# Layer 0 of a two-layer block: the first attention written out by engine, f32 rows for the drives, and drives by TensorE in groups of three

## The chip, the cores and the metric

The kernel is one program on one core of a Trainium2 chip. A core has five engines that each work through a queue of their own and wait for one another by semaphores: TensorE (PE in the profile), VectorE (DVE), ScalarE (ACT), GpSimd (POOL), and SyncE (SP), which issues the DMAs. The metric is the time of one execution on the device, in microseconds (us), as the median of several runs. The two versions differ in the first half of the program only.

## The reference

The input x has 4 blocks (b) of 128 tokens with 128 features. Two layers follow each other, each with three residual parts. Only the first two parts of layer 0 bear on the change:

```
x = x + xattn(layernorm(x), ctx, ctx, Wq, bq, Wk, ..., Wo, bo)      # 16 heads of 8 features
    scores = Q K^T / sqrt(8);  masked: head i sees only the keys j with (j - i) % 16 == 0
    out = softmax(scores) V @ Wo.T + bo
x = x + ssm(layernorm(x), W_in, conv_w, conv_b, W_x, W_dt, b_dt, A_log, D, W_out)
    xi, res = split(x @ W_in);   u = silu(causal_conv4(xi) + conv_b)  # 256 channels
    dbc = u @ W_x                         # 8 columns for dt, 16 for B, 16 for C
    delta = softplus(dbc[dt] @ W_dt + b_dt)
    h[n] = exp(delta * A[n]) * h[n] + delta * u * B[n]        # 16 states n, along the tokens
    y = sum_n C[n] * h[n] + u * D;   out = (y * silu(res)) @ W_out
```

After them come a feed-forward part with ternary weights, and layer 1 with a gated cross-attention, a self-attention with a bias, and a quantised feed-forward part. Their code and order are the same in both versions.

## The kernel before, in words

All 512 tokens fit one core. Each engine's queue is written out in Python, in one function per engine, with a `wait_ge` on a named semaphore ahead of an instruction where it needs another engine's result. So the order on every engine is fixed by the code.

**First attention.** Because of the mask each head sees every 16th key of a block's context, 128 keys, so a block has 16 heads of 128 queries by 128 keys: four groups of four heads, and a group's scores ("strip", 128x512 f32) fill one bank of PSUM. A strip goes through six steps: PE makes the scores (`scores`, L1299), DVE takes the maximum of each head (L889) and subtracts it (`difference`, L897), PE turns the four heads (`turn_diff`, L1402), ACT takes the exponential (L578). When the four strips of a block are done, PE multiplies by the values and by ones (`heads`), ACT makes one over the sum by Ln and Exp (L584, L588), DVE scales (`scaled`, L884), PE projects, and DVE adds to x, normalises and so on. `attention(ph)` is one function per engine that both layers use; it counts steps t, one strip each, and stages are due at fixed distances (`LAG`, `VALUES`, `SCALE`, `PROJECT`, `ADD`, `RSTD`, `NORM`, `TURN`). In layer 0 PE makes two strips of scores at every second step, into a ring of five banks. Ahead of each block's `heads` it multiplies ones with ones six times (`keep_warm(FILLS["heads"], 5)`), whose result nothing reads. Convolution and gates of the SSM come from the table `CHANNELS` in steps 17 to 21 and behind the attention.

**From dbc to the first scan.** PE makes the 40 rows of dbc in bank 6 (dt, B and C). ACT copies the dt rows (L651), PE multiplies them with W_dt, ACT takes Abs with the bias b_dt, Exp and Ln, DVE adds the bias once more (L1022), makes delta (L1025) and delta times u (du, L1028). POOL makes delta and du of the second half of the channels (L485, L488). The rows of B are spread over 128 partitions by a product with a one-hot column. For that they are split in three bf16 parts, by ACT (L653) and DVE (L1017, L1018), while PE multiplies ones 16 times.

**The loop.** 16 states n times two halves hf of the 256 channels make 32 steps k. DVE scans along the tokens (L1054). The scan needs the decay exp(delta A[n]) from ACT (L690) and the drive delta u B[n] in a bank. The drive is made either by DVE, du times the spread rows of B (L1035), or by PE as four transposes (L1576) of du that ACT has scaled token by token, four instructions per state, into one of two buffers (L676). `BY_PE` names the states of the second kind: 4, 5, 7, 8, 9, 11, 12, 13, 15. POOL multiplies the state with C[n] (the read, L496), and PE adds that into y by a product with the identity (L1299).

## Time and profile before

| | us |
|---|---|
| median of 3 runs | 236.97 (236.45 to 237.11) |
| the profiled execution | 236.94 |
| its span (first to last instruction) | 235.1 |
| PE, DVE, ACT, POOL busy | 200.7, 172.6, 119.7, 88.3 |
| mean granted clock of PE | 0.977 |
| first attention, from the first maximum to the last scaled block | 11.2 to 52.2 |
| to the last row of dbc | 62.1 |
| to the first scan | 69.3 |
| to the last scan's end | 113.9 |

The stages follow one another: the convolution of a block needs its attention, dbc needs all of u, the loop needs dbc. Within a stage the engines pass strips or steps to one another. So a stage is read by itself: which engine has no idle time in it, and what ends the waits of the others. The granted clock is a share of full speed, 1.00 being 2.4 GHz and about half of it 1.2 GHz.

### The profile page before, as it was taken

The numbers are of one execution on the slowest core, as the hardware profiler recorded it, in microseconds if no ns is written. First come the engines' busy times: TensorE is split into PE (matmuls) and PEld (weight loads), VectorE is DVE, ScalarE is ACT, GpSimd is POOL, SyncE is SP. The second block draws the span as 40 slices with busy tenths as digits, with TensorE's granted clock in tenths as the row PEclk, the third lists the DMA queues.
The fourth block names the chain that finished last, engine by engine and source line by source line (L and its number), as shares of the span: only waits on it lengthen the run. The fifth ranks groups of instructions, "written<-read, shape, count | busy, mean of one in ns | idle before, by whom it ended". The sixth has DMA issues, their size and how long they took to land.

```text
span 235.1 us, 5061 instructions
## 1 busy us (share of the span) xinstructions
PE 200.7 (85%) x1868; PEld 141.3 (60%) x1868; DVE 172.6 (73%) x486; ACT 119.7 (51%) x292; POOL 88.3 (38%) x104
## 2 busy tenths in 40 slices
PE   8879998799997799999986679999988798876832
PEld 5568777688663245454463446867885776664421
DVE  2489485733399999999789879497775868816785
ACT  3343633435878897986065636335242344453431
POOL 7002408110047799998423064400002566522000
PEclk9999999999999999999999999999999999997696
DMA  6999950000079988300000001400000000000001
GB/s 213 389 427 409 418 242 4 3 0 0 8 216 377 233 96 96 56 1 0 0 3 0 0 0 50 133 0 3 0 0 3 0 4 3 3 3 3 0 0 45
DMA packets 9224, 20.23 MB, mean 86 GB/s; under 512 B 736, under 2 KB 5472, under 8 KB 8176
## 3 DMA queue, kind: packets, MB, share of 16 engines
q1 hardware_dynamic: 8912, 19.78, 27.2%
q8 instruction: 15, 0.25, 0.4%
q10 hardware_dynamic: 288, 0.13, 0.2%
q14 instruction: 9, 0.07, 0.1%
HBM read 17.52 MB, written 2.38 MB: 85 GB/s over the span
## 4 chain that ended last, share of the span: by engine, by line
PE 39%; POOL 17%; DVE 16%; issue 16%; ACT 7%; DMA 3%; SPq 1%; POOLq 0%; DVEq 0%; ACTq 0%
PE bank L1299 32%; POOL region L496 9%; POOL diff L520 6%; DMA ctx_T_sb<-ctx_T 3%; PE bank L1723 3%; PE bank L1402 2%; DVE diff L897 1%; DVE ext L1260 1%; DVE ext L1261 1%; DVE neg_max L889 1%; DVE region L1275 1%; PE bank L1316 1%; ACT region L676 1%; POOL region L485 1%; DVE region L1129 1%
## 5 line engine op out<-in xcount | busy, mean ns | idle before, releaser
L1054 DVE TENSOR_TENSOR_SCAN region<-region,bank 128x512 f32<-128x512 f32 x32 | 37.1, 1203 | 0.9 <-ACT region L690 0.8
L1299 PE MATMUL bank<-region,early_sb 128*128 128x512 f32 x64 | 33.8, 621 | 3.2 <-POOL region L496 2.1
L578 ACT ACTIVATE region<-bank 128x512 f32<-128x512 f32 x32 | 18.6, 594 | 21.7 <-PE bank L1402 21.5
L1299 PE MATMUL bank<-ones 128*128 128x256 bf16 x198 | 28.5, 300 | 1.1 <-POOL ones L432 1.0
L1299 PEld LDWEIGHTS bank<-ones 128*128 128x128 bf16 x198 | 20.6, 107 | 8.0 <-issue 2.2
L536 ACT ACTIVATE lnv<-mv,eps_col 128x1 f32<-128x1 f32 x24 | 7.0, 291 | 31.6 <-DVE mv L819 21.2
L690 ACT ACTIVATE region<-region,a_neg 128x508 f32<-128x508 f32 x32 | 21.1, 708 | 2.3 <-DVE region L1054 1.2
L1402 PE MATMUL bank<-early_sb,diff 128*128 128x128 f32 x128 | 18.8, 280 | 3.8 <-POOL diff L520 3.2
L1299 PE MATMUL bank<-ctx_T_sb,region 128*32 128x128 f32 (+1 forms) x160 | 20.7, 341 | 1.1 <-DMA ctx_T_sb<-ctx_T 0.7
L520 POOL TENSOR_TENSOR diff<-region,neg_max 128x512 f32<-128x512 f32 x15 | 15.5, 1044 | 12.4 <-DVE neg_max L908 12.4
L453 POOL TENSOR_TENSOR xb<-x,rows_sb 128x512 f32<-128x512 f32 x3 | 3.8, 1266 | 39.0 <-DVE x L1179 27.9
L1299 PEld LDWEIGHTS bank<-region,early_sb 128*128 128x128 f32 x64 | 9.8, 189 | 13.8 <-POOL region L496 13.0
L1402 PEld LDWEIGHTS bank<-early_sb,diff 128*128 128x128 f32 x128 | 14.0, 141 | 6.7 <-POOL diff L520 4.1
L908 DVE CUSTOM_DVE_ANT_0 region<-bank,region 128x128 f32<-128x128 f32 x64 | 14.4, 286 | 3.6 <-PE bank L1299 3.6
L1299 PE MATMUL bank<-k_T,region 32*128 32x128 f32 x256 | 15.1, 283 | 2.2 <-ACT k_T L550 1.0
L676 ACT ACTIVATE region<-region,b_tok 128x256 f32<-128x256 f32 x36 | 15.3, 495 | 2.5 <-PE bank L1576 2.5
L1299 PEld LDWEIGHTS bank<-region,ctx_sb 128*128 128x128 f32 x128 | 15.2, 192 | 1.9 <-issue 1.9
L1299 PEld LDWEIGHTS bank<-k_T,region 32*128 32x128 f32 x256 | 12.7, 186 | 5.3 <-ACT k_T L592 1.7
L1204 DVE COPY region<-bank 128x512 f32<-128x512 f32 x16 | 10.9, 686 | 6.6 <-PE bank L1723 6.5
L1299 PE MATMUL bank<-region,ctx_sb 128*128 128x128 f32 x128 | 15.6, 275 | 0.0
L1576 PEld LDWEIGHTS bank<-early_sb,region 128*128 128x128 f32 x72 | 9.0, 141 | 9.1 <-issue 8.1
L889 DVE TENSOR_REDUCE neg_max<-bank 128x4 f32<-128x512 f32 x16 | 10.3, 684 | 3.5 <-PE bank L1299 3.5
(234 smaller groups left out, 412.1 us busy)
## 6 DMA issues: line engine op xcount, KB each, us to landing
ctx_sb<-ctx SPq DMA_DIRECT2D x4, 1024.0 KB, 23.9
ctx_T_sb<-ctx_T SPq DMA_DIRECT2D x3, 1024.0 KB, 10.3
late_sb<-late SPq DMA_DIRECT2D x1, 2416.0 KB, 17.3
bias_scratch<-bias_vec SPq DMA_DIRECT2D x1, 2040.0 KB, 25.3
ctx_T_sb<-ctx_T SPq DMA_DIRECT2D x2, 512.0 KB, 5.9
diff<-c_scratch SPq DMA_DIRECT2D x4, 256.0 KB, 6.2
x<-c_scratch SPq DMA_DIRECT2D x4, 256.0 KB, 6.4
region<-bias_scratch SPq DMA_DIRECT2D x1, 1024.0 KB, 5.6
```

Source lines behind the costliest of these rows:

```text
L496: done(pool.tensor_tensor(read[:, k % 3, :], state[:, k % 3, :], c_rows(n), ALU.mult), "read")
L520: done(pool.tensor_tensor(diff[:, w % 4], neg_biased[:, t % 3], neg_max[:, w % 4, :, None].to_broadcast([P, HG, P]), ALU.subtract), "diff")
L578: done(act.activation(probs_T[:, w % (2 * NG)].rearrange("p h q -> p (h q)"), step_bank(w)[:, :], ACT.Exp, scale=1.0 if w < 16 else -1.0), ...
L676: ins = act.activation(du_B[:, i % 2, b].rearrange("p h c -> p (h c)"), du_T[:, b].rearrange("p h c -> p (h c)"), ACT.Copy, scale=b_tok[:, ...
L690: done(act.activation(dst, src, ACT.Exp, scale=a_neg[:, hf, n:n + 1]), "decay")
L889: done(dve.tensor_reduce(neg_max[:, w % 4, :], step_bank(w)[:, :].rearrange("p (h k) -> p h k", h=HG), AX, ALU.max, negate=True), "neg_max")
L908: ins = dve.tensor_tensor_reduce(neg_biased[:, t % 3, j, :], src[:, j, :], rel_bias[:, HG * g + j, :], -1.0, HIGHEST, ALU.add, ALU.min, ne ...
L1054: done(dve.tensor_tensor_scan(state[:, k % 3, :], decay[:, k % NDA, :], bank[3 + k % 3][:, :], 0.0, ALU.mult, ALU.add), "state")
L1204: done(dve.tensor_copy(p2_T[:, w % 4].rearrange("p c q -> p (c q)"), bank[4 + w % 2][:, :]), "p2T_sb")
L1299: return pe.matmul(dst, lhsT, rhs, start=start, stop=stop)
L1402: ins = pe.transpose(step_bank(w)[:, j * P:j * P + P], diff[:, w % 4, j, :], ident)
L1576: ins = pe.transpose(bank[3 + k % 3][:, b * P:b * P + P], du_B[:, BY_PE.index(n) % 2, b, hf, :], ident)
```

## The change

Three parts of layer 0 are changed; nothing behind the loop is.

**1. The first attention.** `attention(ph)` is split. `second_attention` is the old loop for layer 1. `first_attention` is written out on PE, ACT and DVE, call by call. The scores of a block are made four strips at a time (`scores(0, t, NG)`), into the banks of `FIRST_BANKS`, and as soon as all but the last two strips of the block before have been through ACT. The 24 fills ahead of `heads` are gone. Convolution and gates are made block by block (`convolved(b, hf)`, `gates(b)`, products of 128 columns), those of block 0 ahead of the last block's heads. The sums over weights come later, their maxima behind the attention.

On PE, where the scores of block 1 stand: `k_T` are the keys, `diff` is a strip less its maximum, `ones` are fills, `v_heads` the values. Before:

```order
L1299 MATMUL bank<-k_T,region 128x128 [waits s_probs_T_sb,s_q_heads,s_k_sb]
L1299 MATMUL bank<-k_T,region 128x128 x7
L1402 MATMUL bank<-early_sb,diff 128x128 [waits s_diff]
L1402 MATMUL bank<-early_sb,diff 128x128 x3
L1299 MATMUL bank<-ones 128x256 [waits s_q_heads]
L1299 MATMUL bank<-ones 128x256 x5
L1299 MATMUL bank<-region,v_heads 32x128 [waits s_ones_heads,s_v_sb,s_probs_T_sb]
L1299 MATMUL bank<-region,v_heads 32x128 x15
L1299 MATMUL bank<-region,ones_heads 32x128 x16
```

The same place in the changed kernel:

```order
L1503 MATMUL bank<-early_sb,diff 128x128 [waits s_diff]
L1503 MATMUL bank<-early_sb,diff 128x128 x3
L1384 MATMUL bank<-k_T,region 128x128 [waits s_probs_T_sb,s_v_sb,s_q_heads,s_k_sb]
L1384 MATMUL bank<-k_T,region 128x128 x15
L1384 MATMUL bank<-region,v_heads 32x128 [waits s_v_sb,s_ones_heads,s_probs_T_sb,s_q_heads]
L1384 MATMUL bank<-region,v_heads 32x128 x15
L1384 MATMUL bank<-region,ones_heads 32x128 x16
```

Sixteen products of scores (four strips) now stand in one piece ahead of the heads of the block before, where eight stood, and the fills between are gone.

**2. dt and the rows of B.** b_dt is added by PE: two products of the identity with the broadcast column of b_dt, 512 columns each, start the banks that the dt products then add to. One f32 copy of the 40 rows (`small`, DVE) takes the place of the copies and of the bf16 parts. delta is one instruction of DVE per half, max(dt, 0) + Ln(...) (`steps_of(hf)`); that of the second half stands inside the loop. On PE, from dbc to the loop, before (`bc_parts` is the tile of the three bf16 parts):

```order
L1299 MATMUL bank<-ones 128x256 x6
L1299 MATMUL bank<-region,late_sb 128x512 [waits s_dt_sb]
L1299 MATMUL bank<-region,late_sb 128x512
L1299 MATMUL bank<-ones 128x256 x16
L1299 MATMUL bank<-bc_parts,one_hot_b 128x512 [waits s_gate_sb,s_consts,s_bc_parts]
L1299 MATMUL bank<-bc_parts,one_hot_b 128x512 [waits s_gate_sb]
```

The same place in the changed kernel (`cols_sb` holds b_dt and the one-hot columns, `region` is `small`):

```order
L1384 MATMUL bank<-ones 128x256 x6
L1384 MATMUL bank<-cols_sb,early_sb 128x512 x2
L1384 MATMUL bank<-region,late_sb 128x512 [waits s_small,s_dt_bias]
L1384 MATMUL bank<-region,late_sb 128x512
L1384 MATMUL bank<-region,cols_sb 128x512 [waits s_gate_sb,s_consts]
L1384 MATMUL bank<-region,cols_sb 128x512 [waits s_gate_sb]
```

The two bias products stand between the fills and the dt products, and the dt products wait for the bias products' own semaphore.

**3. The loop.** DVE's drives are those of states 0 to 3, 7 and 11; PE's are the others: groups of three, three and four. The rows of B for states 0 to 3 are spread by f32 products (K = 32). For states 7 and 11 a DMA on SP's queue brings the row to all partitions, from the copy of B and C in DRAM, into `w_tmp` and `wq_rest`; DVE's drive then has both inputs in SBUF. The first four steps are taken in the order (0,0), (1,0), (0,1), (1,1) (state, half). On DVE, from dbc to the scan of step 3, before (L1035 are drives, L1054 scans):

```order
L1028 TENSOR_TENSOR region<-region 128x512 [waits s_u,s_delta]
L1035 TENSOR_TENSOR bank<-region,bank 128x512 [waits s_b_ps,s_du]
L1054 SCALAR_TENSOR_TENSOR region<-region,bank 128x512 [waits s_decay,s_drive]
L1035 TENSOR_TENSOR bank<-region,bank 128x512 [waits s_b_ps]
L1035 TENSOR_TENSOR bank<-region,bank 128x512 [waits s_b_ps,s_du_rest]
L1054 SCALAR_TENSOR_TENSOR region<-region,bank 128x512 [waits s_decay,s_drive]
L1035 TENSOR_TENSOR bank<-region,bank 128x512 [waits s_state,s_b_ps]
L1054 SCALAR_TENSOR_TENSOR region<-region,bank 128x512 [waits s_decay,s_drive]
L1035 TENSOR_TENSOR bank<-region,bank 128x512 [waits s_state,s_b_ps]
L1054 SCALAR_TENSOR_TENSOR region<-region,bank 128x512 [waits s_read,s_decay,s_drive]
```

The same place in the changed kernel (L1099 is delta, L1105 du, L1117 drives, L1139 scans):

```order
L1105 TENSOR_TENSOR region<-region 128x512 [waits s_u,s_delta]
L1117 TENSOR_TENSOR bank<-region,bank 128x512 [waits s_b_ps,s_du]
L1139 SCALAR_TENSOR_TENSOR region<-region,bank 128x512 [waits s_decay,s_drive]
L1099 SCALAR_TENSOR_TENSOR region<-bank,region 128x512 [waits s_sp_log,s_dt_ps]
L1117 TENSOR_TENSOR bank<-region,bank 128x512 [waits s_b_ps]
L1139 SCALAR_TENSOR_TENSOR region<-region,bank 128x512 [waits s_decay,s_drive]
L1117 TENSOR_TENSOR bank<-region,bank 128x512 [waits s_b_ps,s_du_rest]
L1139 SCALAR_TENSOR_TENSOR region<-region,bank 128x512 [waits s_decay,s_drive]
L1117 TENSOR_TENSOR bank<-region,bank 128x512 [waits s_state,s_b_ps] x2
L1139 SCALAR_TENSOR_TENSOR region<-region,bank 128x512 [waits s_read,s_decay,s_drive]
```

delta of the second half now stands behind the first scan, and two drives stand ahead of the scan of step 3, the second of them on the rows of state 2.

The diff, cut to its core:

```diff
+FIRST_BANKS = (0, 1, 2, 3, 4, 7, 0, 1, 2, 3, 4, 7, 1, 0, 2, 3)
...
-BY_PE = (4, 5, 7, 8, 9, 11, 12, 13, 15)
+def by_hand(t, stage):
+    b = due(t, stage)
+    return b if b is not None and b < BY_HAND else None
+BY_PE = (4, 5, 6, 8, 9, 10, 12, 13, 14, 15)
+BY_SPREAD = BY_B[:4]
+BY_ROWS = BY_B[4:]
+ROWS_AFTER = {5: 7, 9: 11}
...
+                if n in ROWS_AFTER:
+                    m = ROWS_AFTER[n]
+                    if m == BY_ROWS[0]:
+                        sp_.wait_ge(S["w_quant"], 3)
+                    sp_.dma_start(b_rows(m), bass.AP(c_dram, m * T, [[0, P], [1, T]])).then_inc(b_in[BY_ROWS.index(m)], 16)
             sp_.wait_ge(S["bias_sb"], 1)
...
-                    keep_warm(FILLS["heads"], 5)
+                if ph == 0 and b >= 1:
+                    pe.wait_ge(S["x_ready"], b)
                 pe.wait_ge(S["probs_T_sb"], 4 * v + 4)
...
+                if ph == 0 and b >= 1:
+                    pe.wait_ge(S["probs_T_sb"], t - 2)
+                    if b == 1:
+                        pe.wait_ge(S["v_sb"], 1)
                 elif ph == 1 and t == NG:
                     pe.wait_ge(S["probs_T_sb"], 16 + 1)
                 elif ph == 1 and t == NG + 2:
...
+            def first_attention():
+                scores(0, 0, NG)
+                turn_xn(0, 0, 2)
+                pe.wait_ge(S["k_sb"], 2)
+                done(mm(kv_bank(0, 1)[:, 0:P], C("bv").to_broadcast([P, P]), ident), "v_bias_ps")
+                turn_xn(0, 0, 3)
+                turn_values(0)
+                pe.wait_ge(S["xnT_sb"], NB)
+                done(mm(bank[5][:, P:T], E("wqT"), xn_T[:, P:T]), "q_ps")
+                keys_values(1)
+                turn_diff(0)
+                turn_diff(1)
+                turn_values(1)
+                turn_diff(2)
+                turn_diff(3)
+                scores(0, NG, NG)
+                heads(0, 0)
+                keys_values(2)
+                turn_diff(4)
+                turn_diff(5)
+                project(0, 0)
+                turn_values(2)
+                turn_diff(6)
+                scores(0, 2 * NG, NG)
+                keys_values(3)
+                turn_diff(7)
+                turn_diff(8)
+                turn_values(3)
+                turn_diff(9)
+                heads(0, 1)
+                scores(0, 3 * NG, NG)
+                turn_diff(10)
+                turn_diff(11)
+                project(0, 1)
+                heads(0, 2)
+                turn_xn(1, 1, 0)
+                turn_diff(12)
+                turn_diff(13)
+                convolved(0, 0)
+                turn_diff(14)
+                project(0, 2)
+                turn_diff(15)
+                convolved(0, 1)
+                weight_sums()
+                heads(0, 3)
+                turn_xn(1, 1, 1)
+                gates(0)
+                turn_xn(1, 1, 2)
+                convolved(1, 0)
+                project(0, 3)
+                convolved(1, 1)
+                gates(1)
+                convolved(2, 0)
+                gates(2)
+                turn_xn(1, 1, 3)
+                convolved(2, 1)
+                convolved(3, 0)
+                gates(3)
+                convolved(3, 1)
...
-            pe.wait_ge(S["bc_parts"], 2)
-            pe.wait_ge(S["consts"], 2)
+                done(mm(bank[4 + hf][:, :], ident, C("b_dt", hf).to_broadcast([P, T]), True, False),
+                     "dt_bias")
+            pe.wait_ge(S["dt_bias"], DH)
+            pe.wait_ge(S["small"], 1)
+            for hf in range(DH):
+                done(mm(bank[4 + hf][:, :], L("w_dt")[DT_AT:DBC, hf * P:hf * P + P], small[DT_AT:DBC, :], False, True), "dt_ps")
+            pe.wait_ge(S["consts"], 1)
...
             def spread_b(n):
-                i = BY_B.index(n)
-                if i >= 2:
-                    pe.wait_ge(S["drive"], DH * (i - 1) + (i == 2))
+                if n >= 2:
+                    pe.wait_ge(S["drive"], n + 1)
                 else:
-                    pe.wait_ge(S["gate_sb"], len(SSM_GROUPS))
-                done(mm(bank[spread_bank(n)][:, :], one_hot_b[0:3 * BC, n:n + 1].to_broadcast([3 * BC, P]),
-                        bc_parts[:, :]), "b_ps")
+                    pe.wait_ge(S["gate_sb"], DH + 1)
+                done(mm(bank[spread_bank(n)][:, :], C("one_hot", n)[B_AT:DT_AT].to_broadcast([BC, P]), small[B_AT:DT_AT, :]), "b_ps")
             def tokens_of_b():
...
-                n, hf = k // DH, k % DH
-                if k == 1:
+                n, hf = unit(k)
+                if k in (1, 2):
+                    spread_b(k + 1)
+                if k == 2:
                     turn_du(1)
-                if hf == 0 and n + 2 in BY_B:
...
-            for hf in range(DH):
+            def decayed(hf):
                 act.wait_ge(S["dt_ps"], hf + 1)
-                done(act.activation(sp[:, hf, 0, :], bank[4 + hf][:, :], ACT.Abs, bias=C("b_dt", hf)), "sp_abs")
-            for hf in range(DH):
-                act.wait_ge(S["sp_abs"], hf + 1)
-                link(act.activation(sp[:, hf, 2, :], sp[:, hf, 0, :], ACT.Exp, scale=-1.0))
-                done(act.activation(sp[:, hf, 1, :], sp[:, hf, 2, :], ACT.Ln, bias=1.0), "sp_exp")
+                link(act.activation(sp[:, hf, 0, :], bank[4 + hf][:, :], ACT.Abs))
+                done(act.activation(sp[:, hf, 2, :], sp[:, hf, 0, :], ACT.Exp, scale=-1.0), "sp_exp")
+            def logarithm(hf):
+                act.wait_ge(S["sp_exp"], hf + 1)
+                done(act.activation(sp[:, hf, 1, :], sp[:, hf, 2, :], ACT.Ln, bias=1.0), "sp_log")
+            decayed(0)
+            logarithm(0)
+            decayed(1)
...
-                link(dve.tensor_tensor(bc_rest[0:end, :], rest[0:end, :], bc_parts[0:end, :], ALU.subtract))
-                done(dve.tensor_copy(bc_parts[0:end, :], bc_rest[0:end, :]), "bc_parts")
-                dve.wait_ge(S["bc_parts"], 1 if end > BC else 2)
-            for hf in range(DH):
-                dve.wait_ge(S["sp_abs"], hf + 1)
-                done(dve.tensor_scalar(du[:, hf, :], bank[4 + hf][:, :], C("b_dt", hf), 0.0, ALU.add, ALU.max), "dt_base")
-            dve.wait_ge(S["dt_base"], 1)
-            dve.wait_ge(S["sp_exp"], 1)
-            done(dve.tensor_tensor(delta[:, 0, :], du[:, 0, :], sp[:, 0, 1, :], ALU.add), "delta")
+            done(dve.tensor_copy(small[B_AT:DBC, :], bank[6][B_AT:DBC, :]), "small")
+            weight_inverses()
+            def steps_of(hf):
+                dve.wait_ge(S["dt_ps"], hf + 1)
+                dve.wait_ge(S["sp_log"], hf + 1)
+                done(dve.scalar_tensor_tensor(delta[:, hf, :], bank[4 + hf][:, :], 0.0, sp[:, hf, 1, :], ALU.max, ALU.add),
+                     "delta_rest" if hf else "delta")
+            steps_of(0)
             dve.wait_ge(S["delta"], 1)
-            dve.wait_ge(S["u"], DH * (len(SSM_GROUPS) - 1) + 1)
+            dve.wait_ge(S["u"], DH + 1)
...
             def drive(k):
-                n, hf = k // DH, k % DH
-                dve.wait_ge(S["b_ps"], BY_B.index(n) + 1)
+                n, hf = unit(k)
+                if n in BY_SPREAD:
+                    dve.wait_ge(S["b_ps"], n + 1)
+                    b_of = bank[spread_bank(n)][:, :]
+                else:
+                    dve.wait_ge(b_in[BY_ROWS.index(n)], 16)
+                    b_of = b_rows(n)
                 if k >= 3:
                     dve.wait_ge(S["state"], k - 2)
-                done(dve.tensor_tensor(bank[3 + k % 3][:, :], du[:, hf, :], bank[spread_bank(n)][:, :], ALU.mult), "drive")
+                done(dve.tensor_tensor(bank[3 + k % 3][:, :], du[:, hf, :], b_of, ALU.mult), "drive")
             dve.wait_ge(S["du"], 1)
             drive(0)
             for k in range(NS * DH):
                 if k == 1:
+                    steps_of(1)
+                    drive(1)
+                elif k == 2:
+                    dve.wait_ge(S["du_rest"], 1)
                     drive(2)
-                    dve.wait_ge(S["du_rest"], 1)
-                    drive(1)
-                if k >= 2 and k + 1 < NS * DH and (k + 1) // DH not in BY_PE:
+                elif k == 3:
+                    drive(3)
+                if 3 <= k < NS * DH - 1 and (k + 1) // DH not in BY_PE:
                     drive(k + 1)
                 if k // DH in BY_PE:
                     dve.wait_ge(S["drive_pe"], DH * BY_PE.index(k // DH) + k % DH + 1)
                 else:
-                    dve.wait_ge(S["drive"], 3 if k == 1 else drives_before(k) + 1)
+                    dve.wait_ge(S["drive"], drives_before(k) + 1)
                 dve.wait_ge(S["decay"], k + 1)
                 if k >= 3:
```

## Rows read from the trace of the kernel before

**Rows 1.** Windows: length, busy PE, PEld, DVE, ACT, POOL; PEclk, DMA share, GB/s.

```profile
11.20:52.20 41.00, 36.85 (x590) 30.00 (x591) 28.37 (x63) 17.47 (x53) 10.29 (x15) 1.00 0.54 222
52.20:62.10 9.90, 9.39 (x71) 8.62 (x70) 2.23 (x9) 6.51 (x15) 0.74 (x2) 1.00 0.01 2
62.10:69.30 7.20, 7.17 (x38) 3.91 (x37) 6.27 (x11) 5.68 (x10) 1.32 (x1) 1.00 0.49 136
69.30:113.90 44.60, 40.75 (x158) 20.14 (x155) 43.76 (x45) 35.11 (x69) 39.81 (x33) 1.00 0.57 121
```

**Rows 2.** Groups by line, 11.2 to 52.2: count, busy us, mean ns, idle before.

```profile
L889 DVE TENSOR_REDUCE neg_max<-bank 128x4 f32<-128x512 f32 x16 | 10.3, 684 | 3.5 <-PE bank L1299 3.5
L897 DVE TENSOR_TENSOR diff<-bank,neg_max 128x512 f32<-128x512 f32 x16 | 10.2, 683 | 0.0
L578 ACT ACTIVATE region<-bank 128x512 f32<-128x512 f32 x16 | 9.2, 593 | 10.2 <-PE bank L1402 10.2
L1299 PE MATMUL bank<-ones 128*128 128x256 bf16 x24 | 3.3, 273 | 0.2 <-DVE x L952 0.2
```

**Rows 3.** DVE's timeline, the last scaling: start, us, idle before and releaser.

```profile
52.23 0.29 DVE L884 TENSOR_TENSOR attn_T<-bank,inv_sum 128x128 f32<-128x128 f32 x1 [3.40 <-ACT inv_sum L588]
```

**Rows 4.** PE's timeline, heads, turns, convolution; scores of layer 1.

```profile
32.90 1.08 PE L1299 MATMUL bank<-region,v_heads 128*32 128x128 f32 x32
38.07 1.04 PE L1402 MATMUL bank<-early_sb,diff 128*128 128x128 f32 x8
54.42 1.95 PE L1299 MATMUL bank<-region 128*128 128x128 f32 x16
179.31 1.17 PE L1299 MATMUL bank<-k_T,region 32*128 32x128 f32 x32 [0.37 <-ACT k_T L592]
```

**Rows 5.** Timelines from dbc to the first scan: PE, ACT, DVE, POOL.

```profile
62.77 1.98 PE L1299 MATMUL bank<-region,late_sb 8*128 8x512 f32 x4
63.93 0.69 ACT L656 ACTIVATE region<-bank,cols_sb 128x512 f32<-128x512 f32 x1 [0.49 <-PE bank L1299]
65.37 0.62 ACT L659 ACTIVATE region<-region 128x512 f32<-128x512 f32 x1
67.84 0.69 DVE L1028 TENSOR_TENSOR region<-region 128x512 f32<-128x512 f32 x1
67.98 1.68 POOL L485 TENSOR_TENSOR region<-region 128x512 f32<-128x512 f32 x1 [15.04 <-ACT region L660]
```

**Rows 6.** Timelines in the loop: DVE, ACT; last POOL reads, DVE's last product.

```profile
76.92 1.21 DVE L1054 TENSOR_TENSOR_SCAN region<-region,bank 128x512 f32<-128x512 f32 x1
78.63 1.21 DVE L1054 TENSOR_TENSOR_SCAN region<-region,bank 128x512 f32<-128x512 f32 x1
93.18 2.33 DVE L1054 TENSOR_TENSOR_SCAN region<-region,bank 128x512 f32<-128x512 f32 x2 [0.44 <-ACT region L690]
84.91 1.31 ACT L690 ACTIVATE region<-region,a_neg 128x508 f32<-128x508 f32 x2
90.78 1.71 ACT L676 ACTIVATE region<-region,b_tok 128x256 f32<-128x256 f32 x4 [1.73 <-PE bank L1576]
110.68 3.72 POOL L496 TENSOR_TENSOR region<-region,x 128x512 f32<-128x512 f32 x3 [0.43 <-DVE region L1054]
113.97 0.98 DVE L1060 TENSOR_TENSOR region<-region,x 128x512 f32<-128x512 f32 x1
```

**Rows 7.** Windows in layer 1, columns as in rows 1.

```profile
200.00:203.00 3.00, 2.17 (x39) 1.81 (x33) 2.22 (x17) 1.36 (x5) 1.52 (x2) 1.00 0.00 0
211.00:214.00 3.00, 1.13 (x7) 0.75 (x6) 2.23 (x9) 1.88 (x6) 0.00 (x0) 1.00 0.00 0
214.00:221.00 7.00, 5.74 (x22) 3.08 (x22) 3.94 (x16) 2.32 (x5) 1.26 (x1) 0.52 0.01 2
222.00:225.00 3.00, 0.98 (x9) 0.63 (x7) 3.00 (x6) 0.46 (x1) 0.00 (x0) 1.00 0.00 0
```

**Rows 8.** The turns (L1402) alone in a window of rows 7.

```profile
200.00:203.00 3.00, 1.16 (x9) 1.03 (x10) 1.00 0.00 0
```

497 lines of the change are left out of this document (262 added, 235 removed).

## The prediction

> **What bounds the kernel now.** I read the windows by stage first, since the stages of layer 0 follow one another. In the first attention DVE is busy 28.37 of 41.00 us, ACT 17.47, and PE 36.85 [rows 1], but 3.3 us of PE are the 24 fills [rows 2]. So no engine is full: a block goes round PE, DVE, PE, ACT, PE, and what costs is that the round is not overlapped enough. The last block's scaling waits 3.40 us for the end of that round [rows 3]. Up to dbc PE is the bound (9.39 of 9.90). From dbc to the first scan it is a chain over ACT and DVE of 7.20 us; PE's 7.17 there are mostly fills. In the loop DVE is busy 43.76 of 44.60 [rows 1]: 32 scans at a distance of 1.12 (two take 2.33, one 1.21), and 0.59 more wherever DVE makes the drive itself (76.92 to 78.63). The rest is waiting for a decay, such as 0.44 at 93.18 [rows 6].
>
> **First attention.** I walk the new order on paper, each instruction at the earliest time at which its queue and its waits allow, with the distances between starts in these rows, and 0.03 to 0.1 us for a hand-over. The longest path, from 11.2:
> - DVE does 8 maxima and differences at 0.60, places values twice (0.27) and does three query products of the same size (0.66, an estimate from these rows): 7.3, to 18.5 (0.68 each, the next starting 0.08 before the end [rows 2]). The heads of block 0 wait for all queries.
> - PE: heads of block 0, 2.0 (two groups like the 1.08 one), keys 1.0. ACT: two copies of keys 0.5, two exponentials 1.1. PE: four strips of scores 1.1 [rows 2, 4]. With hand-overs 24.5.
> - DVE two maxima and a difference 1.9; PE turns two strips and a block of values 1.1 (eight turns take 1.04), heads 2.0, scores 1.1, one strip turned 0.5; ACT two exponentials 1.1; PE heads of block 2, 2.2. To 34.7.
> - ACT Ln, Exp and a copy 0.8. PE convolutions, turns, projection and weight sums 3.5; heads of block 3, 2.2. To 41.4, scaled at 42.1.
>
> Before, the last block is scaled at 52.2: **-10.1**. The fills explain 3.3 at most; the rest is that scores come a whole block earlier. The weakest price is that ACT and PE keep up in the written order: if each of the three later blocks keeps half of its old wait, the gain is 5. That is the other end of this term.
>
> **To dbc.** PE's queue after the last heads: 24 products of convolution, 8 of gates, one projection, at 0.22 (two records each; 16 records take 1.95 [rows 4]) are 7.2, less what the walk starts earlier; the rows of dbc 1.7. From 42.4 to 51.3: 9.2 us after the scaling, where it was 9.9. **-0.7**.
>
> **dbc to the first scan.** The copy of dt on ACT goes; it is replaced by the f32 copy on DVE of the same length, hidden under PE's fills and bias products. The two bias products are on the path: f32, 512 columns, as the two dt products that take 1.98 [rows 5]. They start behind the fills (0.8), and the dt products wait for them: dt starts 2.7 after dbc, where it started 0.65 after. **+2.0**. Against that, ACT did both Abs ahead of the first Exp (63.93 to 65.37), and now does Abs, Exp, Ln of the first half at once: -0.8; and DVE's two L1022 and L1025 become one instruction, -0.4, which before hid under ACT in part. The sum is 8.0 instead of 7.2: **+0.8**. The bf16 split, and PE's 16 fills beside it, lay beside this chain (DVE's L1028 starts as soon as delta is there [rows 5]), so their removal gives nothing. If the bias products lay hidden, this term would be -1.2; if the f32 spread of B (two products, 2.0, as dt) came onto the path as well, +2.0: these are its ends.
>
> **The loop.** Count for DVE: 32 scans x 1.12 = 36.0; 11 drives behind the first scan x 0.59 = 6.5 (13, 7.6, before); delta of the second half 0.7. That is 43.2, where before counts 43.6 and took 44.6. So two drives less save 0.4 net of delta. But waits come:
> - Start. delta of the second half stands behind the first scan. POOL's du (1.3), its first read (1.24, on the same queue behind it), PE's product of y, the spread of state 2 queued behind that product on PE (0.9 each, as the dt products) and the drive on it follow one another, and step 3's scan stands behind that drive on DVE's queue. 5.2 us, against 4.3 that DVE has to do meanwhile: **+0.9**.
> - Groups. For a state driven by PE, ACT needs four scalings and two decays, 1.60 + 1.22 = 2.82 (1.71 and 1.31 less 0.1 where the next starts [rows 6]), and DVE needs 2.25 for its two scans. Each such state puts ACT 0.57 behind. At a state driven by DVE it wins back up to 2.2 (DVE 3.42, ACT 1.22), but only as far as two buffers of scaled du allow: at 90.78 it waits 1.73 for one [rows 6]. Before, the groups are two, three, three and one, with 0.8 of waits for decays; now three, three and four. ACT enters the first group late (it still copies du of the second half), so I get waits of 0.45, 0.55, 0.3, 0.3 and 0.75 at steps 8, 10, 18, 26 and 28: 2.4, **+1.6**.
> - The drives of states 7 and 11 have both inputs in SBUF. DVE's last product of the loop has them too: it started while POOL's last read had 0.43 to go and took 0.98, where the same form took 0.69 ahead of POOL; there POOL's L485 took 1.68, where three reads in a row take 3.72 [rows 5, 6]. So whichever comes second waits. POOL is busy 39.81 of 44.60 [rows 1]. Of the two drives of a state the first comes behind POOL's read, as the product at 113.97 did, and the second ahead of one, since scans are 1.71 apart there: 2 x 0.3 on DVE, **+0.6**; 0 if all come ahead, 4 x 0.9 if all come as POOL starts. The Trainium skill has this rule, "SBUF — State Buffer", "Who interferes with whom": a DVE instruction with two SBUF inputs and a GpSimd one that reads SBUF exclude each other, and the later one is held until the other is done. The trace agrees, with 0.98 for 0.69; by the rule alone a drive that starts with a read would be held for all of it, 4 x 1.2.
>
> In sum -0.4 + 0.9 + 1.6 + 0.6 = **+2.7**; the ends are -0.4 (all waits hidden) and +5.7. The B rows of those states come by two DMAs of 256 KB, queued after the C rows of states 5 and 9; the DMA share in the loop is 0.57 [rows 1] and they are wanted 15 us later: nothing.
>
> **Sum.** -10.1 - 0.7 + 0.8 + 2.7 = -7.3. Walked in the same way, the order of before ends its last scan 1.1 us early, so such a walk misses waits; of that I give back 0.4. -6.9 against the profiled execution's own 236.94 (span 235.1 and 1.8 around it) is 230.0; the median shown is 0.03 higher. **230.0**. Behind the loop the order is the same, so a shift there stays a shift.
>
> **Rivals.**
> 1. The clock falls at the loop's start. PE has only fills and then a wait of about 2.5 us for the first read. The clock fell to 0.52 behind a stretch with PE busy 1.13 of 3.00, but stayed at 1.00 in one with 0.98 [rows 7], so the rows bear out either. At half speed the products of y and the turns of du take twice as long until it rises: +1.7, 231.7. Chance 0.25.
> 2. The attention keeps half of its waits (5 instead of 10.1): 235.1. For it: one late strip now delays a whole block of scores. Against it: each wait above has a price in the rows. Chance 0.13.
> 3. Slower: the clock stays low in the attention. On the path above PE does 16.7 us; at half speed as much again, less what it hides, +14.5: 244.5. It decides from about half of the attention on, since 6.9 of 14.5 eats the whole gain. Against it, the 33.5 us of real work, now in 30, leave PE no emptier than before, when the clock was 1.00 throughout [rows 1]. Chance 0.04. The Trainium skill has a rule for it, "TensorE: Matmul & The Clock Gate", "Part 4: PE-mode transpose": transposes do not count as activity in the way that products do. By it the turns here (64 instructions), with no fills between them, would not hold the clock, and the time would be that of this rival. The trace speaks against it: from 200 to 203 the turns are 1.16 of 2.17 us of work, and the clock is 1.00 [rows 7, 8].
> 4. Nothing changes, because something else ends the attention, such as the context's DMAs. But no wait of PE on a DMA stands in its window; 237.0, chance 0.02.
>
> **Numbers.** Likeliest case 0.56, with 228.4 to 231.4 as its own range (half of the way to the ends of the dt and loop terms); rivals 0.25, 0.13, 0.04, 0.02. The range that holds 8 in 10 takes in the first two cases, with room below for waits that are hidden and above towards the second rival: 227.8 to 232.9. A measurement of this kernel can tell 0.3% (0.7 us). Faster 0.94, same 0.02, slower 0.04.
>
> **What would show it.** The last block's scaling near 42.1; dbc near 51.3; the first scan near 59.3, with PE's two 512-column bias products right ahead of dt; the last scan's end near 107, with DVE waiting for ACT's decays in groups of three and at step 3 for a drive. It is wrong if the granted clock falls below 1.00 before 60, if the four scalings stand as far apart as before, or if the loop takes less than before's 44.6.

## The result and the profile after

The changed kernel takes 235.32 us (median of 20 executions, 231.38 to 238.18), the kernel before 237.13 (20 executions, 236.18 to 241.73). The ratio is 0.985 (95% interval 0.981 to 0.988); it leaves out the executions that count as slow, 11 of the 20 of the changed kernel, which the medians keep (by them it is 0.992). So the changed kernel is faster by more than the noise, but by less than 2%: the medians differ by 1.8 us where 7 were forecast, and 235.32 lies above the range, which ended at 232.9. The profiled execution took 234.37 (span 232.6). By stage, with a second execution of the same kernel that is told of below (run a_5):

| us | before | forecast | after, profiled (234.37) | a_5 (236.44) |
|---|---|---|---|---|
| first maximum starts at | 11.2 | 11.2 | 12.0 | 11.3 |
| to the last scaling of the attention | 41.0 | 30.9 | 31.9 | 32.4 |
| to the rows of dbc | 9.9 | 9.2 | 9.6 | 9.6 |
| to the first scan | 7.2 | 8.0 | 8.2 | 8.2 |
| to the last scan's end | 44.6 | 47.3 | 48.3 | 52.0 |
| from there to the end | 121.2 | 121.2 | 122.6 | 121.3 |

The windows of the changed kernel for the stages of [rows 1], columns as there (length; busy PE, PEld, DVE, ACT, POOL; granted clock; DMA share and GB/s):

```profile
12.00:43.90 31.90, 28.72 (x558) 24.29 (x558) 26.75 (x62) 17.65 (x51) 5.69 (x8) 1.00 0.67 277
43.90:53.40 9.50, 9.26 (x74) 8.52 (x74) 3.34 (x10) 6.41 (x13) 5.36 (x9) 1.00 0.01 2
53.40:61.60 8.20, 6.95 (x28) 3.36 (x28) 3.12 (x7) 4.12 (x9) 0.00 (x0) 1.00 0.48 153
61.60:109.90 48.30, 42.77 (x164) 21.19 (x164) 44.41 (x44) 36.33 (x74) 41.09 (x32) 1.00 0.55 117
```

In the attention DVE is now busy 26.75 of 31.90, where it was 28.37 of 41.00: nearly the same work, with 5.2 us of waits in place of 12.6. The clock stays at 1.00 with the fills gone. In the loop DVE has only 0.65 more to do, and waits 3.9 instead of 0.8. DVE's timeline there (start, length, line, form, and in brackets the idle time ahead and what ended it):

```profile
67.01 0.68 DVE L1117 TENSOR_TENSOR bank<-region,bank 128x512 f32<-128x512 f32 x1
68.24 0.70 DVE L1117 TENSOR_TENSOR bank<-region,bank 128x512 f32<-128x512 f32 x1 [0.56 <-PE bank L1384]
68.84 1.21 DVE L1139 TENSOR_TENSOR_SCAN region<-region,bank 128x512 f32<-128x512 f32 x1
...
74.42 2.33 DVE L1139 TENSOR_TENSOR_SCAN region<-region,bank 128x512 f32<-128x512 f32 x2 [0.36 <-DVE bank L1117]
77.24 2.33 DVE L1139 TENSOR_TENSOR_SCAN region<-region,bank 128x512 f32<-128x512 f32 x2 [0.48 <-issue]
80.05 3.44 DVE L1139 TENSOR_TENSOR_SCAN region<-region,bank 128x512 f32<-128x512 f32 x3 [0.48 <-PE bank L1707]
83.41 1.00 DVE L1117 TENSOR_TENSOR bank<-region,w_tmp 128x512 f32<-128x512 f32 x1
...
91.31 3.44 DVE L1139 TENSOR_TENSOR_SCAN region<-region,bank 128x512 f32<-128x512 f32 x3 [0.73 <-ACT region L723]
...
102.55 2.33 DVE L1139 TENSOR_TENSOR_SCAN region<-region,bank 128x512 f32<-128x512 f32 x2 [0.73 <-ACT region L723]
105.37 4.55 DVE L1139 TENSOR_TENSOR_SCAN region<-region,bank 128x512 f32<-128x512 f32 x4 [0.48 <-PE bank L1707]
```

Three kinds of loss stand in these lines: the drive that waits for the spread of state 2 (68.24), waits of scans from step 6 on, most of them inside the groups of PE's states (74.42, 77.24, 80.05, 91.31, 102.55 and 105.37, that is steps 6, 8, 10, 18, 26 and 28: 3.3 in sum), and a drive of 1.00 with both inputs in SBUF (83.41), which takes 0.67 elsewhere. The tail behind the loop has the same order as before, but takes 1.4 longer in this execution; its clock is 0.86 between 130 and 140 us, and of the traces of this order those without that fall, and without another ahead of 200 us, have tails of 120.9 to 121.3.

### The profile page after: what moved, and what is told of

It reads as the page before. It is cut to its first block, busy times and chain, and to the rows that moved or that the text cites. A ratio compares the mean times of both kernels' runs of the same rounds, so it can differ in the third digit from the quotient of the medians.

```text
span 232.6 us, 5040 instructions
## 1 busy us (share of the span) xinstructions
PE 196.0 (84%) x1857; PEld 137.4 (59%) x1857; DVE 169.6 (73%) x480; ACT 119.7 (51%) x290; POOL 88.2 (38%) x103
## 4 chain that ended last, share of the span: by engine, by line
PE 39%; issue 19%; POOL 19%; DVE 13%; ACT 4%; DMA 3%; SPq 1%; POOLq 0%; DVEq 0%; ACTq 0%
PE bank L1384 31%; POOL region L506 12%; POOL diff L530 6%; DMA ctx_T_sb<-ctx_T 3%; PE bank L1854 3%; PE bank L1503 3%; DVE ext L1345 1%; DVE ext L1346 1%; PE bank L1405 1%; ACT region L748 1%; DVE region L1214 1%; DVE region L1360 1%; DVE region L909 1%; ACT region L788 1%; DVE region L1189 1%
## 5 line engine op out<-in xcount | busy, mean ns | idle before, releaser
L1139 DVE TENSOR_TENSOR_SCAN region<-region,bank 128x512 f32<-128x512 f32 x32 | 37.2, 1203 | 3.4 <-ACT region L723 1.5
L1384 PE MATMUL bank<-region,early_sb 128*128 128x512 f32 x64 | 34.3, 623 | 5.5 <-POOL region L506 4.0
L1384 PE MATMUL bank<-ones 128*128 128x256 bf16 x158 | 23.5, 309 | 2.3 <-ACT b_tok L727 1.3
L1384 PE MATMUL bank<-ctx_T_sb,region 128*32 128x128 f32 (+1 forms) x160 | 21.8, 346 | 2.3 <-DMA ctx_T_sb<-ctx_T 1.6
L1384 PEld LDWEIGHTS bank<-ones 128*128 128x128 bf16 x158 | 16.7, 110 | 7.5 <-ACT b_tok L727 2.1
L530 POOL TENSOR_TENSOR diff<-region,neg_max 128x512 f32<-128x512 f32 x15 | 15.5, 1044 | 12.4 <-DVE neg_max L942 12.4
L709 ACT ACTIVATE region<-region,b_tok 128x256 f32<-128x256 f32 x40 | 16.9, 495 | 2.9 <-PE bank L1707 2.9
L1707 PEld LDWEIGHTS bank<-early_sb,region 128*128 128x128 f32 x80 | 9.9, 141 | 10.6 <-issue 10.3
L1289 DVE COPY region<-bank 128x512 f32<-128x512 f32 x16 | 10.9, 685 | 7.1 <-PE bank L1854 6.9
L1249 DVE TENSOR_REDUCE row_max<-bank 128x1 f32<-128x512 f32 x16 | 10.9, 688 | 2.5 <-PE bank L1384 2.3
L788 ACT ACTIVATE region<-bank,shift 128x512 f32<-128x512 f32 x16 | 10.8, 686 | 3.0 <-DVE shift L1256 3.0
## 6 DMA issues: line engine op xcount, KB each, us to landing
late_sb<-late SPq DMA_DIRECT2D x1, 2416.0 KB, 17.6
```

The lines of the kernel that those rows point to most:

```text
L530: done(pool.tensor_tensor(diff[:, w % 4], neg_biased[:, t % 3], neg_max[:, w % 4, :, None].to_broadcast([P, HG, P]), ALU.subtract), "diff")
L709: ins = act.activation(du_B[:, i % 2, b].rearrange("p h c -> p (h c)"), du_T[:, b].rearrange("p h c -> p (h c)"), ACT.Copy, scale=b_tok[:, ...
L788: done(act.activation(p2[:, b % 2, g, :], bank[g][:, :], ACT.Exp, bias=shift[:, b:b + 1], accum_out=part_sum[:, b, g:g + 1]), "p2")
L1139: done(dve.tensor_tensor_scan(state[:, k % 3, :], decay[:, k % NDA, :], bank[3 + k % 3][:, :], 0.0, ALU.mult, ALU.add), "state")
L1249: done(dve.tensor_reduce(row_max[:, b, g:g + 1], bank[g][:, :], AX, ALU.max), "row_max")
L1289: done(dve.tensor_copy(p2_T[:, w % 4].rearrange("p c q -> p (c q)"), bank[4 + w % 2][:, :]), "p2T_sb")
```

## The experiments

"First six steps" is the time from the start of scan 0 to that of scan 6 (11.0 us before, 12.8 in the profiled execution after); "steps 6 to 31" that from the start of scan 6 to that of scan 31 (32.4 and 34.3).

**The fills of before** (b_nofills):

```diff
-                    keep_warm(FILLS["heads"], 5)
```

> The kernel before without the 24 fills ahead of the heads; nothing else. If the attention's gain comes from the order (four strips of scores in one piece), the stretch from the first maximum to the last scaling loses at most the fills' own 3.3 us of 41, so it stays above 37.7. If the fills were what cost, it falls near the changed kernel's 31.9. If they held the clock, the granted clock falls to about half between 12 and 50 us and the stretch grows by 10 or more.

Measured, one execution: 244.68, with the first maximum at 14.0 (late DMAs) and 44.0 us for the attention instead of 41.0. The clock was 0.5 between 10 and 20, behind a wait of PE for the late DMAs, and 0.74 between 45 and 50: it fell at 47.4, in a wait of PE of 1.97 us ahead of a block's heads, where six fills stood before. So taking the fills out does not bring the old order near 31.9: 9.5 us of the stretch ran at half speed, and with half of that given back it would still take 39.2 (an estimate). The gain of the attention is the order's, but for what the fills' own 3.3 us may be worth. What the fills cost or hold in the old order can't be told from this execution: b_nocover below, which keeps them, started as late (13.4, at half speed until 17.6) and took 42.8.

**The start of the loop** (a_start):

```diff
-            keep_warm(FILLS["dt_in"], 1)
             for hf in range(DH):
                 done(mm(bank[4 + hf][:, :], ident, C("b_dt", hf).to_broadcast([P, T]), True, False), "dt_bias")
-            pe.wait_ge(S["dt_bias"], DH)
-            pe.wait_ge(S["small"], 1)
-            for hf in range(DH):
+                pe.wait_ge(S["dt_bias"], hf + 1)
+                pe.wait_ge(S["small"], 1)
                 done(mm(bank[4 + hf][:, :], L("w_dt")[DT_AT:DBC, hf * P:hf * P + P], small[DT_AT:DBC, :], False, True), "dt_ps")
...
-                if k in (1, 2):
-                    spread_b(k + 1)
+                if k in (0, 1):
+                    spread_b(k + 2)
```

> The changed kernel with two orders on PE altered: no fills ahead of the bias products and bias, dt, bias, dt instead of bias, bias, dt, dt; and the rows of states 2 and 3 spread one product of y earlier. If the bias products and the fills are on the path as I priced them, dbc to the first scan falls from 8.18 to about 6.2. If the spread behind the first product of y holds step 3, the distance from step 2's scan to step 3's falls from 2.97 to about 1.9. Rival: both only wait for something else (POOL's du, ACT's Exp) and neither stretch changes by over 0.3. If the fills held the clock, it falls below 1.00 between 54 and 66.

Measured: 232.92; dbc to the first scan 6.75 (1.4 less, where 2.0 were expected), step 3 after 2.31 instead of 2.97 (0.66 less, where 1.1 were). So both stretches are on the path, at some two thirds of the price. But the clock was 0.50 from 64 to 70, and step 5 came after 5.29 instead of 1.71; since this run also lacks the fills ahead of the bias products, it can't tell whether they had held it.

**The port of SBUF** (a_spread): states 7 and 11 spread by PE at steps 10 and 18.

```diff
-BY_SPREAD = BY_B[:4]
-ROWS_AFTER = {5: 7, 9: 11}
+BY_SPREAD = BY_B
+ROWS_AFTER = {}
+SPREAD_AT = {10: 7, 18: 11}
```

> The changed kernel with the rows of B of states 7 and 11 spread by PE into a bank, as those of states 0 to 3, instead of by DMA into SBUF: their four drives have one input in SBUF. If the port of SBUF shared by VectorE and GpSimd is the cause, the two drives of 1.00 go back to 0.68 and POOL's reads beside them lose no 0.95 each; the loop then falls from 48.3 by 0.6 (the drives alone) to 2 (if POOL's 1.9 are on the path). Rival: PE is the bound in the loop, and two products of 0.9 more on PE make it longer by 0.5 to 1.8.

Measured: 237.44; the clock fell at the loop's start again (0.5 from 63.9 to 77.6, first six steps 17.1). Behind it, steps 6 to 31 take 33.6 instead of 34.3. POOL's timeline of the changed kernel, and of this one:

```profile
83.82 3.43 POOL L506 TENSOR_TENSOR region<-region,k_T 128x512 f32<-128x512 f32 x2
```

```profile
86.21 1.28 POOL L508 TENSOR_TENSOR region<-region,k_T 128x512 f32<-128x512 f32 x1
87.67 1.27 POOL L508 TENSOR_TENSOR region<-region,k_T 128x512 f32<-128x512 f32 x1 [0.19 <-DVE region L1141]
```

The same two reads take 3.43 in one piece there, and 1.28 and 1.27 here, and the first drive of a state goes from 1.00 to 0.67. So each side is held by the other, as the Trainium skill has it ("SBUF — State Buffer", "Who interferes with whom"). On the path it is 0.7, close to the 0.6 forecast.

**A third buffer of scaled du** (a_buf3):

```diff
-        du_B = turn("ssm", [2, NB, DH, P])
+        du_B = turn("ssm", [3, NB, DH, P])
...
-                if i >= 2:
-                    act.wait_ge(S["drive_pe"], DH * (i - 1))
+                if i >= 3:
+                    act.wait_ge(S["drive_pe"], DH * (i - 2))
```

> The changed kernel with three buffers of scaled du instead of two. If ACT's waits of 1.48 at 88.9 and 100.2 for a buffer are what make DVE wait 0.73 at 91.3 and at 102.6, those go and the loop falls from 48.3 to 46.9 or less; DVE's waits at steps 8 and 10 (0.48 each) stay, since there ACT is late from the start. Rival: ACT's 2.82 us per state against DVE's 2.25 is the bound whatever the buffers, and the waits only move: the loop changes by less than 0.5.

Measured: 236.85, the clock at 0.66 between 65 and 80 (first six steps 15.5). Steps 14 to 31 take 21.64 instead of 22.68, steps 6 to 13 are unchanged at 11.6: the buffers' waits were real, and are 1.0.

**The unchanged changed kernel again** (a_again five rounds, a_third, a_4, a_5, a_6 one execution each).

> The changed kernel unchanged, to see a second trace of it and its times beside the next two on one chip. If the clock at the loop's start is what spreads its times (231.4 to 238.2), times lie in two bands some 3 us apart, and a trace of the upper band shows the granted clock at 0.5 between 60 and 75 us and 15 to 17 us for the first six steps, one of the lower band 1.00 and 12.8. Rival: the spread comes from the start (DMA landings, 1 to 2 us) or from the tail's clock, and the first six steps are 12.8 in either.

> The changed kernel unchanged once more, one execution, for its trace. If the clock at the loop's start makes the upper band of its times, this execution is either near 232 with 12.8 us for the first six steps, or near 235 to 238 with the granted clock at 0.5 between 60 and 80 and 15 to 17 us for them. Rival: a time near 235 or above with 12.8 and a clock of 1.00 there.

> The changed kernel unchanged, one execution. Theory: executions above 235 have the granted clock at 0.5 somewhere between 60 and 80 and 15 or more for the first six steps; those below have 12.8. Rival: the upper band comes from the tail's clock (130 to 230) and the start alone, with 12.8 in each.

> As the run before it: above 235 only with a fall of the clock between 60 and 80, by the theory; above 235 with 12.8 us for the first six steps, by the rival.

> As the two runs before it: a third execution for the same question.

Measured: a_again 235.53 (median of 6, 232.15 to 241.47; before 238.30 on that chip, ratio 0.980, 0.971 to 0.989). The traced executions took 232.15, 233.30, 236.63, 236.44 and 233.07. In those of 232.15, 233.30 and 233.07 the first six steps take 12.8 and the clock is 1.00 there; in those of 236.63 (a_4) and 236.44 (a_5) they take 15.3 and 16.5, and the clock falls. The windows of the profiled execution first, then those of a_5:

```profile
64.00:66.00 2.00, 0.00 (x0) 0.00 (x0) 1.94 (x3) 1.84 (x4) 2.00 (x3) 1.00 1.05 363
66.00:70.00 4.00, 3.97 (x8) 1.18 (x8) 3.44 (x5) 0.00 (x0) 2.44 (x2) 1.00 1.05 393
70.00:76.00 6.00, 5.29 (x19) 2.34 (x19) 5.64 (x8) 5.07 (x11) 4.09 (x4) 1.00 0.92 185
```

```profile
64.00:66.00 2.00, 0.23 (x1) 0.23 (x2) 1.97 (x3) 1.59 (x3) 2.00 (x3) 1.00 1.03 370
66.00:70.00 4.00, 4.00 (x5) 1.07 (x5) 2.12 (x4) 0.00 (x0) 2.19 (x2) 0.55 1.05 397
70.00:76.00 6.00, 6.00 (x11) 2.26 (x10) 3.88 (x6) 1.64 (x4) 2.54 (x2) 0.50 0.91 167
```

PE is idle or nearly so from 64 to 66 in both; in a_5 the clock is then at half speed, PE is full, and DVE and ACT wait for it (3.88 and 1.64 busy of 6.00, where they are 5.64 and 5.07). What PE does in that stretch of a_5 is the chain on the path (products of y, the spreads of states 2 and 3, the turn of du):

```profile
65.78 1.50 PE L1384 MATMUL bank<-region,early_sb 128*128 128x512 f32 x2 [2.37 <-POOL region L506]
67.20 2.07 PE L1384 MATMUL bank<-region,cols_sb 32*128 32x512 f32 x2
69.20 2.08 PE L1384 MATMUL bank<-region,early_sb 128*128 128x512 f32 x2
71.21 2.07 PE L1384 MATMUL bank<-region,cols_sb 32*128 32x512 f32 x2
73.21 1.12 PE L1698 MATMUL bank<-early_sb,region 128*128 128x128 f32 x4
```

The same products in the profiled execution:

```profile
66.03 1.12 PE L1384 MATMUL bank<-region,early_sb 128*128 128x512 f32 x2 [2.37 <-POOL region L506]
67.08 1.12 PE L1384 MATMUL bank<-region,cols_sb 32*128 32x512 f32 x2
```

Each pair takes 2.07 where it takes 1.12 at full speed. Behind the same wait of 2.37 the clock falls or does not: it falls in 2 of 6 traced executions of this kernel, and in a_spread and a_buf3, which have its order up to there. In the traces of this kernel it separates the times of 236.4 and more from those of 234.4 and less. It is not all of that difference: in a_4 the loop takes 2.4 longer, but the tail behind it takes 124.2, 3.3 more than in the trace of a_again, with two more falls (at 138 and 182). And most of the 20 times of the result have no trace, and do not lie in two bands with a gap between them. So the expected theory, that all executions above 235 are explained by the loop's start, is not shown.

**Work in that wait** (a_warm), and before without its cover (b_nocover):

```diff
             turn_du(0)
+            pe.wait_ge(S["duT_sb"], 1)
+            keep_warm(11, 1)
             for k in range(NS * DH):
```

> The changed kernel with 11 fills on PE in its wait for the first read of the loop (1.1 us of the 2.4). If the fall of the clock there is what the changed kernel loses in most executions, the granted clock stays 1.00 from 55 to 80, the first six steps take 12.8, and the median lies 1.5 to 3 below that of the changed kernel. Rival: 11 fills are not what the clock answers to, or it falls elsewhere as often: same median within 0.7.

Measured on the chip of a_again: 232.48 (231.06 to 235.60), 3.05 less than the median of a_again, ratio to before 0.973 (0.966 to 0.980). With six executions each, ranges that overlap, and ratios to before (0.980 and 0.973) whose intervals overlap, the 3.05 is not clear of noise by itself. Its trace has the clock at 1.00 and 12.85 for the first six steps:

```profile
64.00:66.00 2.00, 2.00 (x9) 0.87 (x7) 1.97 (x3) 0.38 (x1) 2.00 (x3) 1.00 1.05 402
66.00:70.00 4.00, 4.00 (x12) 1.28 (x10) 3.43 (x5) 0.53 (x2) 2.25 (x2) 1.00 1.05 387
```

The clock is also 1.00 from 64 to 80 in the traces of a_groups, a_turn and a_top below, which have work in this wait too. Of the nine traces without it (six of the changed kernel, a_start, a_spread and a_buf3) five have the fall there.

```diff
-            keep_warm(FILLS["bc_parts"], 7)
...
             pe.wait_ge(S["b_tok"], 1)
-            keep_warm(FILLS["loop"], 1)
```

> The kernel before without the 16 fills ahead of the spreads and the 12 ahead of the first turn of du. If these were what kept the clock at the start of its loop, the granted clock falls there (65 to 80 us) in most executions, its first six steps take 13 to 15 instead of 11.0, and its median rises by 1 to 3. Rival: before is safe because its wait for the first read is short (1.2 us), and nothing changes but the few tenths that the fills themselves may cost.

Measured: 237.81 (before 238.30, ratio 1.000, 0.995 to 1.005). A miss, and a telling one: the clock did fall in the one traced execution (0.5 from 68.8 to 75.6), but the first six steps took 11.03 as ever.

```profile
69.00:75.00 6.00, 5.25 (x11) 2.17 (x12) 5.83 (x10) 4.86 (x9) 3.01 (x3) 0.50 0.78 267
75.00:80.00 5.00, 4.02 (x15) 1.80 (x13) 4.97 (x7) 3.99 (x8) 3.72 (x3) 0.94 1.04 376
```

In the order of before the slow stretch here falls on products that hold up no scan (the bf16 spreads, the skip products and the first turn of du, from 69.8 to 75.8, around the first scan at 73.2), and DVE is busy nearly all the time. So the changed order does not only make room for the fall, it also puts y and the spread of state 2 on the path where it falls.

**The groups, and ACT's late entry** (a_groups: the fills, the spreads by PE and the nine states of before; a_turn):

```diff
-BY_PE = (4, 5, 6, 8, 9, 10, 12, 13, 14, 15)
+BY_PE = (4, 5, 7, 8, 9, 11, 12, 13, 15)
+SPREAD_AT = {8: 6, 16: 10, 24: 14}
```

> The kernel with fills and with the rows of DVE's states spread by PE, but with the nine states of before driven by PE (groups of two, three, three and one; DVE drives 0 to 3, 6, 10 and 14). If the groups of three, three and four cost 1.6 as I forecast, steps 6 to 31 take about 32.4, as before, where the same spread with groups of three, three and four took 33.6. Rival: the loss there is ACT's late start alone, which the groups share: 33.3 or more.

Measured: 233.35; steps 6 to 31 take 33.9, against 33.6 with groups of three, three and four (a_spread). So the longer groups are no loss in sum. But the two runs differ in more than the groups: here DVE also makes two drives more behind step 6, 1.2 us at 0.59. Its waits there are 2.3 in all, against 3.1 in a_spread. So the longer groups cost some 0.8 of waits and pay for it with the two drives that they save. Against the 32.4 of before, with the same groups and drives, two waits of the late entry (0.36 and 0.48, steps 6 and 8) and two for spreads by PE (0.30 and 0.28) make up most of the 1.5.

```diff
             turn_du(0)
+            pe.wait_ge(S["duT_sb"], 1)
+            keep_warm(6, 1)
+            turn_du(1)
             for k in range(NS * DH):
...
-                if k == 2:
-                    turn_du(1)
```

> The changed kernel with the turn of du's second half ahead of PE's first product of y instead of behind the second, and 6 fills ahead of it (the small rows lie in another tile, so that the scaled du may be written that early). If ACT's late entry into the first group is what makes DVE wait at steps 6, 8 and 10 (0.45, 0.57, 0.57), ACT starts its first scaling some 5 us earlier and steps 6 to 13 take 10.1 to 10.6 instead of 11.6. It also covers the wait in which the clock fell: 1.00 from 55 to 80, median as with the 11 fills less 1. Rival: ACT's 2.82 us per state bounds the group however early it starts: 11.3 or more.

Measured: 231.69 (230.63 to 233.92, ratio 0.978, 0.969 to 0.988). The loop takes 47.2 instead of 48.3: step 6 comes 0.45 earlier, steps 6 to 13 take 10.9 instead of 11.6, between what was expected (10.1 to 10.6) and the rival's 11.3. ACT now enters the first group at 65.9, where it did at 72.0, and the clock is 1.00 up to 207 in the trace.

**All together** (a_best: a_warm with a_start, a_spread and a_buf3; a_top: a_turn with those three, and the fills of before kept ahead of the first bias product).

> All edits together: the fills in the wait, bias and dt alternating without fills ahead (1.4 less up to the first scan), the spread of state 2 earlier (0.66 less at step 3), rows of states 7 and 11 spread by PE (0.7 less in the loop), three buffers (1.1 less). They lie in different stretches, so 3.9 in sum below the kernel with fills alone: 228 to 230. Rival: PE, with the spreads on it, and ACT then bound the loop and half of it is lost: 231.

> That early turn together with three buffers, the spreads by PE, the earlier spread of state 2, and bias and dt alternating with the fills of before ahead of them. Terms: dbc to the first scan 8.18 to 7.4; step 3 2.97 to 2.3; steps 6 to 31 34.3 to about 31.5; no clock fall before 100. In sum some 4.3 below the kernel with fills alone: median 228.5, and below both kernels of the case. Rival: with more work on PE in the loop PE becomes the bound: steps 6 to 31 stay at 33, 230.

Measured: a_best 231.74 (228.66 to 233.70, ratio 0.965, 0.957 to 0.973), above the 228 to 230 expected; its trace has the clock at 0.5 from 56.9 to 63.7, ahead of the cover, and 16.35 for the first six steps. a_top **230.69** (227.95 to 235.65, ratio 0.966, 0.958 to 0.974), the best median here and 7.6 below before on that chip, though 2.2 above the 228.5 expected. dbc to the first scan takes 7.3, the first six steps 11.7, the loop 45.7. Steps 6 to 31 take 32.8, near the rival's 33 and not the 31.5 expected: what a_turn, a_buf3 and a_spread saved there one by one (0.7, 1.0 and 0.7) comes to 1.5 together. PE is busy 44.4 of the loop's 45.7, as the rival has it; that PE is the bound was not tried further.

## Why the prediction was wrong

In sign and place it was right; the size was wrong. Two steps failed. The first is the clock: the likeliest case had it at full speed behind the attention, with a fall at the loop's start as a rival of +1.7 (chance 0.25), and the tail as fixed ("a shift there stays a shift"). The second is the size of single terms, above all the loop's waits and the last block of the attention.

The profiled execution, in which the clock holds in the loop, splits by the stage table: it starts 0.8 later, the attention takes 1.0 more than forecast, the way to dbc and to the first scan 0.35 and 0.2, the loop 1.0 and the tail 1.4. That is 4.75, less the 0.4 that the forecast had given back: 234.37 for 230.0. So three of the four traced executions without a fall in the loop (232.15, 233.07, 233.30 and 234.37) already lie above 232.9, and the fall comes on top.

- **First attention, -10.1:** measured -9.1 (31.9), and 31.1 to 32.4 us in the other traces of this order. The walk's order of waits held (scalings at 22.3, 31.1, 37.3 and 43.9). What it lacked are gaps on PE, inside the keys of block 3 (in 5 of the 14 traces of this order) and inside the scores of block 3 (in 13 of 14), at the same instruction each time, in which PE waited for nothing that the timeline shows. PE's timeline after:

```profile
25.89 0.86 PE L1384 MATMUL bank<-ctx_T_sb,region 128*32 128x128 f32 x24 [0.27 <-issue]
...
30.33 0.95 PE L1384 MATMUL bank<-k_T,region 32*128 32x128 f32 x24
32.04 0.50 PE L1384 MATMUL bank<-k_T,region 32*128 32x128 f32 x8 [0.76 <-issue]
```

  The second gap is 0.26 to 1.19 in the others. a_6 has neither gap and takes 31.1, 0.2 from the forecast; the traces with the second gap alone take 31.1 and that gap (31.4 with 0.26, 31.9 with 0.76). So most of the miss of this term is that gap. The DMA records of the traces bear on its cause: queue q8 carries packets of the kind "instruction", 16 KB each (15 in the profiled execution, 0.25 MB), and in all 14 traces PE goes on at this instruction 1.2 to 1.5 us behind the end of one of them, wherever between 28.8 and 30.7 that end lies (in a_6 it lies early enough that PE hardly stops). The same holds for the five gaps in the keys (1.3 to 1.5), 126 of PE's records earlier. So the gaps are most likely waits for code; no run varied it. Rival 2, half of the gain, is refuted.
- **dbc, -0.7, and the first scan, +0.8:** measured -0.35 and +1.0. Right to 0.35 and 0.2; a_start shows that the bias products and the fills ahead of them are on the path, with 1.4 of the 8.2.
- **The loop, +2.7:** measured +3.7 with the clock at 1.00. The step that failed is the size of the waits under "Groups". They stand at the steps that were forecast (8, 10, 18, 26 and 28), with 0.48, 0.48, 0.73, 0.73 and 0.48, 2.9 in sum where 2.4 were forecast, and one of 0.36 stands at step 6, which the forecast did not have. Less the 0.8 of before this is +2.5 for +1.6, nearly all that the loop missed. The cause that was given holds: the late entry of ACT is worth 1.1 (a_turn: 0.45 and 0.7), the two buffers 1.0 (a_buf3), and the longer groups some 0.8 of waits, which the drives that they save outweigh (a_groups). The shared port came out as forecast, 0.6: the first drives of states 7 and 11 take 1.00 and 0.99 for 0.67, and a_spread gains 0.7. The start, +0.9, is left with some 1.0.
- **Rival 1, the clock at the loop's start, 0.25 and +1.7:** it has the place that the rival named. It came in 2 of the 6 traced executions of this kernel, where it cost 2.4 and 3.7 (loops of 50.8 and 52.0 for 48.3), and in a_buf3 and a_spread, where the first six steps took 2.6 and 4.3 more. The step that failed is the price: the forecast had the products of y and the turns at half speed, but not that the spreads of states 2 and 3 are on the same chain, and that ACT's entry is pushed out with them. At +1.7 the rival's 231.7 lay inside the range; at 2.4 to 3.7 it would have been 232.4 to 233.7. Its chance of 0.25 was set from one pair of windows that bear out either [rows 7]; 2 of 6 does not show it wrong. How many of the 20 executions had the fall is not known, so neither is its share in the median.
- **Rival 3, a low clock in the attention:** did not come. In no trace of the changed order is the clock below 1.00 between 12 and 50. The rule on transposes that was weighed there finds no support in them: with the 64 turns and no fills the clock held, though the turns stand among many other products.
- **The rest:** the forecast took the tail as fixed, and it was not. From the last scan's end it takes 120.9 to 121.3 in the traces of the changed order where the clock holds up to 200 us, and 122.5 to 124.4 in those where it falls ahead of that, some 27 or 71 us behind the loop's end. This kernel has such a fall in 4 of its 6 traces, worth 1.3 to 3.0 against the 121.2 of before. The tail's code is the same; of the three traces with the order of before two have a fall there too (tails of 121.6 and 123.2), and whether the change makes it likelier is not shown. DMAs let the first maximum start anywhere from 10.5 to 12.0 (13.4 and 14.0 in two traces with the order of before). Both hide differences of a microsecond in single executions.

## What to carry to other kernels

When an edit takes work off an engine, ask what that engine does in the next wait and what stands right behind it: here a wait in which PE did nothing cost twice, once as a wait, and in some executions again, as the clock fell and the products behind it were the ones on the path. Five traces have a few useless products in that wait (11, 1.1 us), or better a real instruction moved into it (the turn of du): four keep the clock there, and in the fifth it fell ahead of them. Price such a fall by all that hangs on the slow products, and not by those products alone. And compare kernels by the stages of several traces, not by one total: here the stages from dbc to the last scan repeat to 0.05 us where the clock holds, while totals spread over nearly 7.
